# Row maxima joined by a reduction instead of an elementwise maximum, a normalisation spread over two heads, and the second layer's first normalisation moved two rounds ahead

## The reference

```python
# layer 0, attention
h = layernorm(x) * (1 + ca) + sa
Q, K = (h @ Wq.T, h @ Wk.T)            # 8 heads of 64
attn = softmax(einsum('bnhr,bmhr->bhnm', Q, K))
x = x + ga * einsum('bhnm,bmhd->bnd', attn, V)
h = layernorm(x) * (1 + cb) + sb       # input of the experts (product keys), then x += gb * experts(h)
# layer 1
h = layernorm(x) * (1 + ca) + sa
xn = h / max(norm(h), 1e-12) * sqrt(128) * gamma
q, kv, a = split(xn @ W_qkva.T); a = sigmoid(a)
y = scan over n of (y = a * y + kv)
x = x + ga * q * y
h = layernorm(x) * (1 + cb) + sb
xr, xk = mixes of h and of h one row earlier
x = x + gb * sigmoid(xr @ W_r.T) * (relu(xk @ W_k.T) ** 2 @ W_v.T)
```

## Time and profile before

| | |
|---|---|
| median of three executions | 3028.55 us (3027.59 to 3028.96) |
| the profiled execution | 3042.62 us |
| its span | 3040.8 us |
| attention, table, experts | up to 2823 us of the span |
| second layer | 2823 to 3038 us of the span |
| TensorE busy in the span | 2775.4 us (91%) |

### The profile page before, as it was taken

One profiled execution on the slowest core, in us unless ns is written; L12 is line 12 of the kernel. 1 busy time (PEld: TensorE's weight loads), 2 busy tenths in 40 slices (PEclk: granted clock), 3 DMA queues, 4 the chain that ended last, 5 costly groups with the idle time before them and its releaser, 6 DMA issues. The chain is left out here.

```text
span 3040.8 us, 77592 instructions
## 1 busy us (share of the span) xinstructions
PE 2775.4 (91%) x27940; PEld 2091.0 (69%) x27940; DVE 2294.6 (75%) x8471; ACT 2180.4 (72%) x4273; POOL 1777.8 (58%) x1756
## 2 busy tenths in 40 slices
PE   5999999999999999999999985799989899998688
PEld 3777777777777777777777774566666666666443
DVE  5676776767767767767767645899999999997565
ACT  3888888887888887887887860566666666665575
POOL 3788887788779878878778770333333333331111
PEclk7999999999999999999999996687777777777799
DMA  3000000000000000000000003000000000000000
GB/s 103 1 1 8 1 1 8 1 1 8 1 1 8 1 1 8 1 1 8 1 1 8 1 8 123 1 0 0 0 0 0 0 0 0 0 0 2 8 21 28
DMA packets 11793, 27.63 MB, mean 9 GB/s; under 512 B 1529, under 2 KB 6137, under 8 KB 11137
## 3 DMA queue, kind: packets, MB, share of 16 engines
q1 hardware_dynamic: 11618, 25.48, 2.5%
HBM read 17.07 MB, written 8.40 MB: 8 GB/s over the span
## 5 line engine op out<-in xcount | busy, mean ns | idle before, releaser
L284 POOL TENSOR_TENSOR probs_l<-probs,probs_h 128x512 fp32r<-128x512 f32 x1024 | 1302.3, 1294 | 342.7 <-ACT probs_h L378 339.0
L377 ACT ACTIVATE probs<-bank 128x512 f32<-128x512 f32 x1024 | 636.0, 621 | 280.3 <-PE bank L698 200.7
L539 DVE TENSOR_REDUCE maxes<-ring 128x1 f32<-128x512 f32 x1024 | 659.7, 686 | 185.0 <-PE ring L678 184.2
L378 ACT ACTIVATE probs_h<-bank 128x512 fp32r<-128x512 f32 x1024 | 636.9, 622 | 0.0
L697 PE MATMUL bank<-q_hh,k_hl 128*128 128x512 f32 x1024 | 425.7, 416 | 1.8 <-ACT probs_h L378 1.6
L698 PE MATMUL bank<-q_lm,k_h 65*128 65x512 f32 x1024 | 406.7, 397 | 0.0
L708 PE MATMUL obank<-probs_h,x_l 128*128 128x512 f32 x1024 | 405.5, 396 | 0.0
L710 PE MATMUL obank<-probs_h,x_h 128*128 128x512 f32 x1024 | 404.5, 395 | 0.0
L709 PE MATMUL obank<-probs_l,x_h 128*128 128x512 f32 x1024 | 403.8, 394 | 0.0
L678 PE MATMUL ring<-k_hl,q_hh 128*128 128x512 f32 x1024 | 339.3, 412 | 12.0 <-DVE maxes L539 7.4
L1074 ACT ACTIVATE low_hot<-obank 128x512 f16<-128x512 f32 x512 | 296.9, 603 | 66.0 <-PE obank L1249 52.9
(11 more groups left out here) (252 smaller groups left out, 4986.2 us busy)
## 6 DMA issues: line engine op xcount, KB each, us to landing
xt<-in_x SPq DMA_DIRECT2D x8, 512.0 KB, 9.5
out_x<-xt SPq DMA_DIRECT2D x8, 512.0 KB, 2.6
x<-out_x SPq DMA_DIRECT2D x1, 4096.0 KB, 12.1
out_x<-x SPq DMA_DIRECT2D x16, 256.0 KB, 2.1
mod<-out_x SPq DMA_DIRECT2D x3, 512.0 KB, 13.7
pk_wq<-in_w_q SPq DMA_DIRECT2D x1, 1024.0 KB, 5.9
pk_wqT<-in_w_qT SPq DMA_DIRECT2D x1, 1024.0 KB, 7.4
hot_rule<-in_hot_rule SPq DMA_DIRECT2D x1, 776.0 KB
```

The lines of the kernel that those rows point to most:

```text
L284: nc.gpsimd.tensor_tensor(probs_l[:, i, :], probs[:, s % 4, :], probs_h[:, i, :].bitcast(F32), ALU.subtract).then_inc(low_ready, 1)
L377: nc.scalar.activation(probs[:, s % 4, :], st[s % 4], ACT.Exp)
L378: nc.scalar.activation(probs_h[:, i, :], st[s % 4], ACT.Exp).then_inc(st_free[s % 4], 1)
L539: nc.vector.tensor_reduce(maxes[:, i, k:k + 1], ring[bank_of(at)][:], AX.X, ALU.max).then_inc(rows_maxed, 1)
```

## The change

Three things change. First, `whole_max` is a `tensor_reduce` over the last axis of `maxes`, in place of a `tensor_tensor` of its two columns; the maximum is the same. Second, `second_norm` is spread: n = 3, 4 stay in head 1 (steps 13, 14), and n = 5 to 8 go to head 2 (steps 13, 14). Third, in the second layer the first norm runs two rounds ahead as far as `normed` (with two buffers for h), `mix_normed` moves from ScalarE's end of round b to VectorE's start of round b+1 as eight `tensor_scalar` with (x - mean) * rstd, so that `second_shift` is gone, TensorE puts `turn_mixed(b-1)` behind the first half of the scan's products, and VectorE puts the variance of the second norm ahead of `floor_norm`.

```diff
@@ attention, VectorE
-                nc.vector.tensor_tensor(row_max[:], maxes[:, :, 0], maxes[:, :, 1], ALU.max).then_inc(max_ready, 1)
+                nc.vector.tensor_reduce(row_max[:], maxes[:], AX.X, ALU.max).then_inc(max_ready, 1)
...
-                        if h == 1 and s >= 13 and not first:
-                            for n in range(2 * (s - 13) + 3, 2 * (s - 13) + 5):
+                        if h == 1 and s in (13, 14) and not first:
+                            second_norm(link, s - 10, b - 1)
+                        if h == 2 and s in (13, 14) and not first:
+                            for n in range(2 * (s - 13) + 5, 2 * (s - 13) + 7):
                                 second_norm(link, n, b - 1)
@@ second layer, GpSimd
             first_rstd(0)
+            first_rstd(1)
             norm_root(0)
             for b in range(B):
+                if b + 2 < B:
+                    first_rstd(b + 2)
                 if b + 1 < B:
-                    first_rstd(b + 1)
                     norm_root(b + 1)
                 second_rstd(b)
@@ second layer, ScalarE
             normed(0)
             modulation_rows()
+            normed(1)
             sums_of_squares(0)
...
                 if scanning:
                     turned_units(b)
+                    decays(b, 0)
                 if mixing:
                     shifted_h(b - 1)
                 if scanning:
-                    decays(b, 0)
-                if ahead:
-                    normed(b + 1)
-                if scanning:
                     decays(b, 1)
+                if b + 2 < B:
+                    normed(b + 2)
...
-                if scanning:
-                    mix_normed(b)
@@ second layer, VectorE
+            def mix_normed(b):
+                dve.wait_ge(rstd2_ready, b + 1)
                 if b:
-                    dve.wait_ge(mixed_ready, 2 * b)
-                moments_of(1, b)
...
+                    dve.wait_ge(mix_turned, 2 * b)
+                for t in range(TB):
+                    made = nc.vector.tensor_scalar(mixed[:, t], x2[:, b * TB + t], mean_var[:, 1, t, 0:1], rstd[:, 1, t:t + 1], ALU.subtract, ALU.mult)
+                    if t % 4 == 3:
+                        made.then_inc(mixed_ready, 1)
...
+            first_moments(1)
+            first_shift(1)
             dve.wait_ge(rows_ready, 4)
             scaled(0)
...
-                if ahead:
-                    first_moments(b + 1)
-                    first_shift(b + 1)
+                if mixing:
+                    mix_normed(b - 1)
+                if b + 2 < B:
+                    first_moments(b + 2)
                 if scanning:
                     scan(b, 0)
-                if ahead:
-                    scaled(b + 1)
+                if b + 2 < B:
+                    first_shift(b + 2)
                 if scanning:
                     scan(b, 1)
-                if ahead:
+                if b + 1 < B:
+                    scaled(b + 1)
                     moved(b + 1)
                 if scanning:
                     add_scanned(b, 0)
                     add_scanned(b, 1)
                     second_moments(b)
-                if ahead:
+                    variance_of(1, var2_ready)
+                if b + 1 < B:
                     floor_norm(b + 1)
-                if scanning:
-                    variance_of(1, var2_ready)
                 if mixing:
                     gated(b - 1, 0)
                     gated(b - 1, 1)
-                if scanning:
-                    second_shift(b)
-                if mixing:
                     add_mixed(b - 1, 0)
                     add_mixed(b - 1, 1)
@@ second layer, TensorE
                 if scanning:
                     turn_units(b)
+                    scan_products(b, 0)
                 if mixing:
                     turn_mixed(b - 1)
                 if scanning:
-                    scan_products(b, 0)
                     scan_products(b, 1)
```

More of the change, by code:

```diff
@@ L1437, in build_second_layer @@
         r_norm = sb("l1_r_norm", [P, TB])
-        h = sb("l1_h", [P, TB, D])
+        h = [sb(f"l1_h{i}", [P, TB, D]) for i in range(2)]
         unit = sb("l1_unit", [P, TB, D])
@@ L1552, in normed @@
                 for t in range(TB):
-                    last = nc.scalar.activation(h[:, t], x2[:, b * TB + t], ACT.Identity, bias=shift[:, 0, t:t + 1], scale=rstd[:, 0, t:t + 1])
+                    last = nc.scalar.activation(h[b % 2][:, t], x2[:, b * TB + t], ACT.Identity, bias=shift[:, t:t + 1], scale=rstd[:, 0, t:t + 1])
                 last.then_inc(normed_ready, 1)
@@ L1560, in sums_of_squares @@
                 for t in range(TB):
-                    last = nc.scalar.activation(unit[:, t], h[:, t], ACT.Square, accum_out=squares[:, t:t + 1])
+                    last = nc.scalar.activation(unit[:, t], h[b % 2][:, t], ACT.Square, accum_out=squares[:, t:t + 1])
                 last.then_inc(squares_ready, 1)
@@ L1566, in unit_rows @@
                 for t in range(TB):
-                    made = nc.scalar.activation(unit[:, t], h[:, t], ACT.Copy, scale=r_norm[:, t:t + 1])
+                    made = nc.scalar.activation(unit[:, t], h[b % 2][:, t], ACT.Copy, scale=r_norm[:, t:t + 1])
                     if t % 4 == 3:
@@ L1578, in decays @@
                 nc.scalar.activation(decay[:, half(k)], ring[k][:], ACT.Sigmoid).then_inc(decay_ready, 1)
[L1580 to L1585, removed]
             def shifted_h(b):
@@ L1607, in _ @@
             for b in range(B + 1):
-                scanning, mixing, ahead = b < B, b > 0, b + 1 < B
+                scanning, mixing = b < B, b > 0
                 if scanning:
                     turned_units(b)
+                    decays(b, 0)
                 if mixing:
@@ L1658, in first_shift @@
                 dve.wait_ge(rstd1_ready, b + 1)
-                shift_of(0).then_inc(shift1_ready, 1)
+                nc.vector.scalar_tensor_tensor(shift[:], mean_var[:, 0, :, 0], -1.0, rstd[:, 0], ALU.mult, ALU.mult).then_inc(shift1_ready, 1)
             def scaled(b):
                 dve.wait_ge(normed_ready, b + 1)
-                link(nc.vector.scalar_tensor_tensor(h[:], row(1, b), 1.0, h[:], ALU.add, ALU.mult))
+                link(nc.vector.scalar_tensor_tensor(h[b % 2][:], row(1, b), 1.0, h[b % 2][:], ALU.add, ALU.mult))
             def moved(b):
-                nc.vector.tensor_tensor(h[:], h[:], row(0, b), ALU.add).then_inc(h_ready, 1)
+                nc.vector.tensor_tensor(h[b % 2][:], h[b % 2][:], row(0, b), ALU.add).then_inc(h_ready, 1)
             def floor_norm(b):
@@ L1684, in second_moments @@
                 dve.wait_ge(x_scanned, 2 * b + 2)
+                moments_of(1, b)
+            def mix_normed(b):
+                dve.wait_ge(rstd2_ready, b + 1)
                 if b:
[L1686 to L1691 removed]
+                    dve.wait_ge(mix_turned, 2 * b)
[3 more added lines that the diff above has]
+                        made.then_inc(mixed_ready, 1)
             def gated(b, k):
```

5 lines of the change are left out of this document (1 added, 4 removed).

## The result

The changed kernel takes 2988.52 us (median of four, 2985.75 to 2992.74) against 3028.76 us (four runs of the kernel before: the three behind the forecast and one of 3040.68 us). The ratio is 0.9859, 95% interval 0.9839 to 0.988: 40 us less, where 44 were forecast (2984). The profiled execution fell from 3042.62 to 2992.74 us, which is 50.

What follows compares the result with a forecast made beforehand. TensorE, busy 2775.4 of 3040.8 us, was taken as the bound, with the second layer's chain through all engines. Terms 24.0 + 0.8 + 13.0 - 1.0 + 7.4 = 44.2 us off 3028.55 gave 2984 us, range 2971 to 3001.

Steps and rivals of the forecast that it cites:

- The reduction: Attention, row_max: takes the low end, 0.23 us, returning 24.0 us from five heads and 0.8 from a sixth wait.
- five in all: Attention, head 0 of batches 2, 3, 5, 6, 7: row_max took 5.16 to 5.17 us, priced at 4.8 each.
- an execution without the profiler has fewer held heads: Rival, attention: three fewer long row_max waits outside the profiler, 14 us less to gain, 2998 us; chance 0.10.
- the number of operands: Attention, row_max: one-operand instructions taken as not held by GpSimd, two SBUF inputs as contending; reduction at the low end.
- The norm over two heads: Attention, second_norm: head 1's wait goes, 7 x 1.86 = 13.0 us gained; head 2 costs 1.0 in all.
- my bound of 7.8: Attention, head 2: the four added operations end at the latest 7.8 us behind row_max's start; TensorE allows 7.15.
- the wait moves to head 2: Rival, attention: head 2's four operations end as late as head 1's did, 13.0 us only moved, 2996 us; chance 0.13.
- the slower case: Attention, head 2: each of four operations held through four subtractions, 95 us lost against 44 gained, 3079 us; chance 0.04.
- The second layer: Second layer: 8.4 us from six periods, 2.6 at the end, less 3.1 and 0.5 at the start: 7.4 us gained.
- The net of a round: Second layer, full periods: 3.08 us of mix_normed leave the chain, 0.88 and 0.8 enter: 1.4 us gained a round.
- the clock: Rival, second layer: less idle time keeps TensorE's clock up, 6 x 1.5 = 9 us more, 2975 us; chance 0.10.
- VectorE did not become the bound: Rival, second layer: the scan waits for mix_normed and statistics on VectorE, 7.4 us not gained, 2991 us; chance 0.10.

Runs made afterwards that it cites:

- layer_filled: Kernel before, TensorE turning the second half of the unit rows four times over each round from the second on: 3026.95 us against 3032.23, ratio 0.9972.
- The copy experiment: Changed kernel with a one-operand float32 copy of one column of the maxima added behind the reduction: 2992.47 us in one profiled run.
- the two kernels with an added instruction: Changed kernel with an unread instruction behind the reduction: the old maximum (2989.01 us against 3021.57, ratio 0.9889) or a copy (2992.47 us, profiled).

## Why the prediction was right, and where it was off

**The forecast of 2984 us in 2971 to 3001 held**; measured 2988.5. The three mechanisms came out as forecast. Two terms were off in size, in opposite directions, and the reasons given for two readings were wrong, so that the total is as close as 4 us is in part luck.

**The reduction** was to take 0.2 us and return 24.8. It takes 0.17, the rounds of head 0 went to 26.5, and in the profiled execution it returned about 26 (39.6 of attention less the 13 of the norm). In executions without the profiler the reduction alone gave 19 us. The step that mis-sized it is the one that counts the held heads, "five in all": five was the count of one execution. In batches 1 to 7, the profiles of other kernels with the old maximum have two (spread norm alone, second layer alone) or four (TensorE filled), and not the same batches. With it went the assumption that the 14.1 us between the profiled execution and the median hold for both kernels: in the changed one it is 2992.74 - 2988.52 = 4.2. A held head costs 4.8 us, so a count that varies fits both, and it fits the wider scatter of kernels with the old maximum (11 to 25 us in six series of 6 to 17 runs, against 2 to 8 us in seven series of 4 to 6 runs where `row_max` is a reduction). No run shows it: each kernel was profiled once, and the 17 times of the kernel before show no steps of 4.8 us. The rival "an execution without the profiler has fewer held heads" thus describes the difference, but nothing supports its cause: the profiled executions of spread norm alone and of the second layer alone are below their medians (3015.26 against 3018.33, 3010.42 against 3014.93).

**Why the reduction is free** I argued from the number of operands, next to a sentence of the Trainium skill on `tensor_reduce` ("SBUF — State Buffer", section "Who interferes with whom"). The copy experiment takes the first away: a single operand was held for 5.13 us. The Trainium skill's sentence gave the right answer; my own reason would have passed a copy or a `tensor_scalar` as well. The trace of the kernel before already spoke against it. Its `var`, a `tensor_scalar` of one operand, takes 0.17 us when free; in two heads 0 it took 1.35, and in seven other places 0.86:

```profile
294.39 1.35 DVE L431 TENSOR_SCALAR var<-mean_var 128x8 f32<-128x8 f32 x1
```

**The end of a hold.** I read in rows 4 and 5 that `row_max` is released when GpSimd runs out. In the two kernels with an added instruction, holds of 5.13 to 5.18 us end although GpSimd goes on at once. In the maximum's hold shown above, which ends at 294.58 us, GpSimd and ScalarE have

```profile
288.27 6.28 POOL L285 TENSOR_TENSOR probs_l<-probs,probs_h 128x512 fp32r<-128x512 f32 x5
294.56 1.29 POOL L285 TENSOR_TENSOR probs_l<-probs,probs_h 128x512 fp32r<-128x512 f32 x1
...
293.79 0.59 ACT L379 ACTIVATE probs_h<-bank 128x512 fp32r<-128x512 f32 x1
```

The five subtractions end at 294.55, and each of them is recorded as starting 0.04 to 0.05 us before the end of the one ahead. The sixth starts 0.01 us behind the fifth, since ScalarE finished its input only at 294.38. All 28 holds of 2.8 to 5.2 us of the old maximum or an added instruction, in six profiles, look like this: the hold ends 0.02 to 0.03 us after the end of a subtraction whose successor starts 0.01 to 3.4 us later, and inside the hold every successor starts 0.03 to 0.06 us before its predecessor's end. The 289 cases in which they took 1.0 to 1.1 us also end with a subtraction that has none right behind it. So a held instruction waited until GpSimd had no next subtraction ready, and its price depends on how far GpSimd is behind ScalarE. What decides whether a head is held at all stays open: in batches 1 to 7 of the kernel before, `row_max` of head 0 always starts 1.07 to 1.09 us into a subtraction of 1.29 with the next one right behind; five were held, and two got in at its end (0.23 and 0.24 us).

**The norm over two heads** was to give 13.0 us and take 1.0. It gives 14 us alone, and takes nothing: in the changed kernel the four operations of head 2 end 5.6 us behind the start of `row_max` in six batches and 5.75 in the seventh, within my bound of 7.8, and ScalarE, not VectorE, is still what `q_and_k` waits for. The rival "the wait moves to head 2" and the slower case are out.

**The second layer** was to give 7.4 us. It gives 13.7 in this pair of profiles. The net of a round came out (21.95 with full clock to 20.50: 1.45 for 1.4). So did the start: the first `floored` comes 17.91 us behind the stage's first statistics instead of 14.79, 3.12 for 3.1, although the terms as I wrote them add up to 2.8, and the 0.25 us of gaps between the instructions stand in none of them. The tail, from the last `floored` to the end of the last store's issue, went from 42.47 to 39.95 us, 2.5 for 2.6; but other profiles have 42.46 to 45.06 for the same code of the old stage and 38.35 to 39.94 for that of the new one, so that closeness is luck. The first period did not come out: 0.5 us longer forecast, 18.45 to 20.27 measured. The clock is in it too. The same code took 18.62 in the profile of the second layer alone, where the stretch has a granted clock of 0.77 and not 0.67:

```profile
2804.80:2825.00 20.20, 10.65 (x28) 5.39 (x28) 12.45 (x44) 10.53 (x36) 3.27 (x2) 0.67 0.00 0
...
2824.80:2843.50 18.70, 8.99 (x28) 4.83 (x28) 12.55 (x45) 10.55 (x37) 3.27 (x2) 0.77 0.00 0
```

What was left out of the sum is the clock, which stood among the rivals at 9 us and 0.10. Five of the six full periods before are 23.35 to 23.80 us and not 21.95, 8.2 us in all, and `layer_filled` shows this without any other part of the change. Of the 8.2 the changed kernel lost 2.2 again in its first two periods (20.27 and 21.35 us). The profile had the answer in part: its one round at a clock of 1.00 took 21.95 us. I should have put the clock's part into the sum, not beside it. My reading that TensorE had idled longer ahead of the round at the lower clock was wrong: it idles 3.0 us in that round and in the one of 21.95 us alike. In the changed kernel it is 20.50 - 18.48 = 2.0 us, with the clock at its upper level. Why one round in six kept its clock before stays open. VectorE did not become the bound: the rounds could still be cut to 19.15 us.

**The errors offset each other** only in part. To the 44.2 us of the sum the profiles add about 6 for the second layer, and the timed runs of the parts take away 5 for the held heads and add 2 for the norm: 47 us, against 40.2 measured. Alone, the three parts gave 19.4, 13.9 and 17.3 us, 50.6 in all. These were taken against a median of 3032.23 us on another chip, and the kernel before has 3021.57 to 3032.23 from chip to chip. The 7 to 10 us that are missing are not accounted for by any run.

## What to carry to other kernels

Price a wait by the period of the work around it: a wait of 3.1 us cost 4.8, and a list of instruction durations over many equal rounds showed both the held ones and the ones that cost nothing. Do not take the number of such events from one profile: here it was five of seven in one and two of seven in another. On VectorE next to a busy GpSimd, a small elementwise instruction on a path that TensorE waits for may be held as long as GpSimd's instructions follow each other without a gap (up to 5.2 us here), as may a copy, while a reduction of the same data was not held once. And where an engine's order has two results ready at nearly the same time, let the one with a further engine behind it go first: moving one 0.2 us instruction ahead of 0.8 us of others was worth 0.75 us in every round.

## What the runs showed that I had not expected

A one-operand float32 copy of eight elements a partition, which takes 0.16 us when free, was held up to 5.17 us by GpSimd's subtractions, like the two-operand maximum, and a `tensor_reduce` of the same tile stood right ahead of it 64 times at 0.16 or 0.17 us. All 28 long holds of the copy and the maximum, old or added, ended at the first subtraction that had no next one ready. Kernels with the same maximum have different heads held in their profiles, two to five of seven, which would be worth 4.8 us each; that the count varies between executions of one kernel is likely and not shown. And in a round with 3.0 us of idle time of TensorE, spells at its lower clock cost 1.6 us more; 12 superfluous transposes, which left 1.9 us of idle time, brought them back.
